# Attention's value products: a step's two of the high part first, the wait for the low part behind them

## The chip, the core and the metric

The kernel runs on one core of one Trainium2 chip. The core has five engines with a queue each: PE (TensorE, matrix products; its weight loads are shown as PEld), DVE (VectorE), ACT (ScalarE), POOL (GpSimd) and SP (SyncE, which here only issues DMAs). An engine takes the instructions of its queue in order, and an instruction waits until the semaphores that it names have reached their values. The metric is the device time of one execution in microseconds (us).

## The reference, cut to what matters

One block of a transformer with conditioning, then a rotation, on x of 4 x 1024 x 576 in float32. The change is in attention: 16 heads of 36 columns, 1024 tokens, four batches, so 64 independent heads.

```python
qkv = h @ W_qkv + b_qkv                     # h: layernorm(x), modulated
q, k, v = (qkv[:, :, 0], qkv[:, :, 1], qkv[:, :, 2])
scores = jnp.einsum('blhd,bmhd->bhlm', q * scale, k)
attn = jax.nn.softmax(scores, axis=-1)
o = jnp.einsum('bhlm,bmhd->blhd', attn, v).reshape(b, l, c)
x = x + gate_msa * (o @ W_proj + b_proj)
```

Around it stand the modulation, the MLP with GELU (576 to 2304 and back) and a rotation of each token by a matrix exponential; the change touches none of them.

## The kernel before, in words

The program runs stage after stage: preparation, q/k/v, attention, projection, MLP, rotation. Attention (`stage_attention`) takes the span from about 650 to 1760 us. Products keep float32's accuracy by splitting an operand into a high part, rounded to the type that PE multiplies, and a low part, the rest; both are multiplied and added up in PSUM.

A head has STEPS = 8 steps. A step handles 256 keys (two tiles of 128) by 512 queries; steps 0 to 3 are the first half of the queries (`lh` 0), 4 to 7 the second. For each head the engines do this:

- PE, `scores` (L1052): two products give the step's scores, keys by queries, into one of two PSUM buffers (`a_psum_t`). The row's maximum is already in the product, through two extra rows of `a_qs`, so its result needs only the exponential. PE runs AHEAD = 3 steps in front with these.
- ACT (L1004, L1006): two exponentials of the buffer, one rounded into `a_ph` (the high part), one in full into `a_pf`, or back into the PSUM buffer in steps 1 and 5. After the second, `exp_done` counts.
- The low part `a_pl` = full less high: POOL does it for steps 0, 2, 3, 4, 6 and 7 (L896, `lo_pool` counts), DVE for steps 1 and 5 (L945, `lo_dve` counts). DVE reads the PSUM buffer, which becomes free for PE's scores two steps on only then (L1045). `a_ph`, `a_pl` and `a_pf` are rings of eight steps.
- PE, `values` (L1071, L1072): four products with the two tiles' values (`a_vs`) as weights, high and low for the first tile, then high and low for the second, all summed in `a_psum_o`. The wait for the low part stands ahead of all four. `p_free` counts when the last is done.
- PE, `score_tile` (L1035): queries by keys of the head after the next, 128 queries by two halves of 512 keys, only to find the maxima; DVE reduces each half (L929), and after tile 7 the pairs to one number a query (L933).
- POOL, `split_max` (L884, L886): splits these maxima, after its low part of step 0; DVE turns them (L940), and SP writes them into the rows of `a_qs` by four DMAs (`put_max`, L800, 2 KB each). PE's scores of a head's step 0 wait for that (`max_in`, L1049). In SP's queue `put_max` stands behind the output of the head before (L822, L823) and one more row copy (L835), and ahead of the loads of a later head (L789, L792).
- DVE copies the head's result out of PSUM (L952, L957).

PE's order in a step is written out: scores of three steps on, values of this step, one score tile. POOL's and DVE's orders are written out too; `heads` runs the body as a loop over four heads at a time (SLOTS = 4), with a branch at its end. Lines in the profile are those of this listing.

Of the kernel before, what the change touches and what calls it, by code (L numbers as in the profile page):

```python
# [37 lines left out]
GT = 512  # L38
# [652 lines left out]
def stage_attention(nc, q_s, k_s, v_s, o_t, sums, ada, gates2, x2_s, rsums, wproj, b_proj, early):  # L691
# [5 lines left out]
    KT = L // P  # L697
    LH = L // GT
    PAIR = 2
    STEPS = LH * KT // PAIR  # L700
# [5 lines left out]
    RING = 8  # L706
# [3 lines left out]
    VW = VLO + D  # L710
# [9 lines left out]
    with ExitStack() as ctx:  # L720
# [6 lines left out]
        vs = sb("vs", [P, SLOTS, KT, VW], F32R)  # L727
        pf = sb("pf", [P, RING, COLS])
        ph = sb("ph", [P, RING, COLS], F32R)
        pl = sb("pl", [P, RING, COLS], F32R)  # L730
# [13 lines left out]
        p_o = ps("o", [P, LH, GT])  # L744
# [12 lines left out]
        exp_done, lo_pool, lo_dve = sem("exp_done"), sem("lo_pool"), sem("lo_dve")  # L757
# [11 lines left out]
        def heads(eng, body):  # L769

            n = NHEAD // SLOTS
            with eng.Fori(0, n - 1) as i:
                for u in range(SLOTS):
                    body(SLOTS * i + u, u, i, False)
            for u in range(SLOTS):
                body(SLOTS * (n - 1) + u, u, n - 1, True)

        def lo_counts(n_heads, s):

            d = sum(x <= s for x in DVE_LO)  # L780
            return NPOOL * n_heads + s + 1 - d, NDVE * n_heads + d

        with nc.Block() as block:
# [226 lines left out]
            @block.tensor  # L1010
            def _(pe):
                pe.sem_inc(p_free, RING)

                def score_product(out, u, t):

                    for h in range(L // 512):
                        m = pe.matmul(out[:, h * 512:(h + 1) * 512], qs[0:SROWS, u, t * P:(t + 1) * P],
                                      ks[0:SROWS, u, h * 512:(h + 1) * 512], start=True, stop=True)
                    m.then_inc(s_ready, 1)

                def lead_tile(n):
                    u, t = divmod(n, KT)
                    if t == 0:
                        pe.wait_ge(qk_in[u], 16 * QK_LOADS)
                    if n >= 3:
                        pe.wait_ge(s_free, n - 2)
                    score_product(lead_slots[n % 3], u, t)

                def score_tile(hd, u, i, t):

                    if t == 0:
                        pe.wait_ge(qk_in[u], 16 * QK_LOADS * (i + 1))
                    for h in range(2):
                        pe.wait_ge(half_free, 2 * (KT * (hd - 2) + t) + h + 1)
                        pe.matmul(p_s[:, h * 512:(h + 1) * 512], qs[0:SROWS, u, t * P:(t + 1) * P],  # L1035
                                  ks[0:SROWS, u, h * 512:(h + 1) * 512], start=True, stop=True) \
                          .then_inc(half_ready, 1)

                def scores(hd, u, i, s):

                    lh, j = divmod(s, PER_LH)
                    if s == 0:
                        pe.wait_ge(max_in[u], START + 64 * (i + 1))
                    if s >= 2 and s - 2 in DVE_LO:
                        pe.wait_ge(lo_dve, lo_counts(hd, s - 2)[1])  # L1045
                    elif isinstance(hd, int) and hd == 0 and s < 2:
                        pe.wait_ge(s_free, LEAD - 2 + s)
                    else:
                        pe.wait_ge(exp_done, STEPS * hd + s - 1)  # L1049
                    for r in range(PAIR):  # L1050
                        t = PAIR * j + r
                        m = pe.matmul(p_t[:, s % 2, r * GT:(r + 1) * GT], ks[0:MROWS, u, t * P:(t + 1) * P],  # L1052
                                      qs[0:MROWS, u, lh * GT:(lh + 1) * GT], start=True, stop=True)
                    m.then_inc(t_ready, 1)

                def values(hd, u, i, s):

                    lh, j = divmod(s, PER_LH)
                    if s == 0:
                        pe.wait_ge(v_in[u], 16 * V_LOADS * (i + 1))  # L1060
                    if j == 0:
                        pe.wait_ge(o_copied[lh], START + hd)
                    n_pool, n_dve = lo_counts(hd, s)
                    if s in DVE_LO:
                        pe.wait_ge(lo_dve, n_dve)
                    else:
                        pe.wait_ge(lo_pool, n_pool)
                    for r in range(PAIR):
                        t = PAIR * j + r
                        cols = slice(r * GT, (r + 1) * GT)  # L1070
                        pe.matmul(p_o[0:VW, lh], vs[:, u, t], ph[:, s % RING, cols], start=(t == 0), stop=False)  # L1071
                        m = pe.matmul(p_o[0:VW, lh], vs[:, u, t], pl[:, s % RING, cols], start=False,  # L1072
                                      stop=(t == KT - 1))
                    m.then_inc(p_free, 1)

                for n in range(LEAD):
                    lead_tile(n)
                for s in range(AHEAD):
                    scores(0, 0, 0, s)
                pe.wait_ge(s_free, LEAD)  # L1080

                def body(hd, u, i, last):
                    for s in range(STEPS):
                        if s + AHEAD < STEPS:
                            scores(hd, u, i, s + AHEAD)
                        elif not (last and u == SLOTS - 1):
                            scores(hd + 1, (u + 1) % SLOTS, i + (u == SLOTS - 1), s + AHEAD - STEPS)
                        values(hd, u, i, s)
                        if not (last and u >= SLOTS - 2):
                            score_tile(hd + 2, (u + 2) % SLOTS, i + (u + 2) // SLOTS, s)  # L1090

                heads(nc.tensor, body)
# [1260 lines left out]
```

## Time and profile before

| | us |
|---|---|
| median of 3 runs | 3061.78 (3058.14 to 3062.56) |
| the profiled execution | 3062.73 |
| its span, first to last instruction | 3061.1 |
| PE busy | 2805.0 (92%) |
| DVE busy | 1680.9 (55%) |
| POOL busy | 1437.3 (47%) |
| ACT busy | 1416.8 (46%) |
| L1071 and L1072, value products, 1024 each | 420.9 and 405.1 |
| L896, POOL's low parts, 384 | 908.6 |

The busy shares are means over stages that differ: ACT and POOL have most of their work in attention. A product's time in the trace runs to its modelled end, and the next one starts before that, so products are counted here by the distance between their starts. A wait is the idle time of an engine just before an instruction, with the instruction that released it.

### The profile page before, as it was taken

What the parts mean: (1) busy time and instruction counts of PE and PEld (TensorE: products, weight loads), DVE (VectorE), ACT (ScalarE), POOL (GpSimd) and SP (SyncE); (2) the same over time, 40 slices, a digit from 0 to 9 for tenths busy, and PEclk for the clock granted to TensorE, in tenths of its full rate; (3) what the DMA queues carried; (4) which work ended last, traced back from release to release, by engine and by line L of the source; (5) the groups of instructions that cost most, each with busy time, mean ns of one, the idle gap of its engine ahead of it and who ended that gap; (6) DMA issues with size and microseconds to landing.
All of it is one profiled execution on the core that took longest, in us unless ns stands there. A gap on an engine that the chain in (4) does not pass through costs nothing. (4 is left out here: it accounts for less than half of the span.)

```text
span 3061.1 us, 51443 instructions
## 1 busy us (share of the span) xinstructions
PE 2805.0 (92%) x16066; PEld 2272.3 (74%) x16066; DVE 1680.9 (55%) x3417; ACT 1416.8 (46%) x1835; POOL 1437.3 (47%) x1073
## 2 busy tenths in 40 slices
PE   7859999969999999999999879689999999999977
PEld 3248878846666666666666568589999999999976
DVE  4446777558999999999999657511111111111126
ACT  2112322229999999999999836511111111111112
POOL 1232333128888888888888836512222222222210
PEclk8769999979999999999999989899999999999989
DMA  5476675653443434343343259892112111211126
GB/s 191 136 245 228 228 249 196 234 170 85 89 93 83 95 81 94 85 90 91 85 96 81 71 165 289 246 310 74 37 38 66 46 38 37 74 38 37 53 74 217
DMA packets 336907, 377.68 MB, mean 123 GB/s; under 512 B 162816, under 2 KB 226952, under 8 KB 336764
## 3 DMA queue, kind: packets, MB, share of 16 engines
q1 hardware_dynamic: 327162, 356.66, 39.0%
q0 software_dynamic: 4224, 9.44, 1.7%
q10 hardware_dynamic: 5382, 9.67, 1.0%
q8 instruction: 95, 1.56, 0.2%
q14 instruction: 44, 0.36, 0.0%
HBM read 225.77 MB, written 158.93 MB: 126 GB/s over the span
## 5 line engine op out<-in xcount | busy, mean ns | idle before, releaser
L896 POOL TENSOR_TENSOR a_pl<-a_pf,a_ph 128x1024 fp32r<-128x1024 f32 x384 | 908.6, 2401 | 24.8 <-ACT a_pf L1006 24.8
L929 DVE TENSOR_REDUCE a_mx<-a_psum_s 128x1 f32<-128x512 f32 x992 | 637.5, 684 | 92.4 <-PE a_psum_s L1035 88.5
L1004 ACT ACTIVATE a_ph<-a_psum_t 128x1024 fp32r<-128x1024 f32 x512 | 525.9, 1027 | 133.6 <-PE a_psum_t L1052 126.5
L1607 POOL TENSOR_TENSOR m_al<-m_af,m_ah 128x256 fp32r<-128x256 f32 x288 | 211.1, 733 | 760.1 <-DVE m_ah L1616 760.1
L1655 PE MATMUL m_psum_h<-m_ht,m_w 128*128 128x256 f32 x4032 | 528.1, 283 | 30.2 <-DMA m_w<-w_s 20.5
L1616 DVE CAST m_ah<-m_af 128x256 fp32r<-128x256 f32 x288 | 85.1, 295 | 830.2 <-ACT m_af L1593 830.2
L1655 PEld LDWEIGHTS m_psum_h<-m_ht,m_w 128*128 128x128 f32 x4032 | 504.3, 189 | 33.7 <-issue 32.9
L1593 ACT ACTIVATE m_af<-m_psum_h,m_bias 128x256 f32<-128x256 f32 x288 | 136.4, 473 | 826.7 <-PE m_psum_h L1655 826.7
L1669 PE MATMUL m_psum_y<-m_w,m_ah 128*128 128x288 f32 x2304 | 506.7, 295 | 1.6 <-DVE m_y L1633 1.5
L1071 PE MATMUL a_psum_o<-a_ph,a_vs 128*100 128x512 f32 x1024 | 420.9, 411 | 22.4 <-POOL a_pl L896 18.9
L1072 PE MATMUL a_psum_o<-a_pl,a_vs 128*100 128x512 f32 x1024 | 405.1, 396 | 0.0
L1006 ACT ACTIVATE a_pf<-a_psum_t 128x1024 f32<-128x1024 f32 x384 | 391.2, 1019 | 0.0
L1669 PEld LDWEIGHTS m_psum_y<-m_w,m_ah 128*128 128x128 f32 x2304 | 388.1, 188 | 3.4 <-DVE m_y L1633 2.8
L1052 PE MATMUL a_psum_t<-a_qs,a_ks 110*128 110x512 f32 x1024 | 337.9, 412 | 37.8 <-DVE a_pl L945 31.3
L1669 PE MATMUL m_psum_y<-m_w,m_al 128*128 128x288 f32 x1152 | 341.3, 296 | 0.0
L1035 PE MATMUL a_psum_s<-a_ks,a_qs 108*128 108x512 f32 x992 | 313.9, 397 | 2.5 <-DVE a_mx L929 2.4
L1071 PEld LDWEIGHTS a_psum_o<-a_ph,a_vs 128*100 128x100 f32 x1024 | 168.7, 165 | 150.1 <-POOL a_pl L896 99.7
L1052 PEld LDWEIGHTS a_psum_t<-a_qs,a_ks 110*128 110x128 f32 x1024 | 184.5, 191 | 122.6 <-DVE a_pl L945 82.9
L663 PE MATMUL q_psum_pqk<-q_ht,q_w 128*128 128x512 f32 x1008 | 257.9, 408 | 13.3 <-DMA q_bv<-in_L_cond_b_qkv_dram 13.3
L1035 PEld LDWEIGHTS a_psum_s<-a_ks,a_qs 108*128 108x128 f32 x992 | 188.3, 190 | 64.9 <-DVE a_mx L929 3.6
L663 PEld LDWEIGHTS q_psum_pqk<-q_ht,q_w 128*128 128x128 f32 x1008 | 188.1, 192 | 55.6 <-issue 13.7
L1669 PEld LDWEIGHTS m_psum_y<-m_w,m_al 128*128 128x128 f32 x1152 | 216.6, 188 | 0.0
(232 smaller groups left out, 3059.5 us busy)
## 6 DMA issues: line engine op xcount, KB each, us to landing
a_qs<-q_s SPq DMA_DIRECT2D x192, 144.0 KB
a_ks<-k_s SPq DMA_DIRECT2D x192, 144.0 KB
w_s<-q_ws SPq DMA_DIRECT2D x64, 324.0 KB, 3.5
h_s<-p_ht SPq DMA_DIRECT2D x40, 512.0 KB, 4.7
m_ht<-h_s SPq DMA_DIRECT2D x16, 1280.0 KB, 8.2
v_s<-q_vo SPq DMA_DIRECT2D x64, 288.0 KB, 2.3
a_vs<-v_s SPq DMA_DIRECT2D x128, 144.0 KB, 4.5
q_s<-q_qko SPq DMA_DIRECT2D x32, 512.0 KB, 2.7
```

What stands on the lines that cost most here:

```text
L663: i = pe.matmul(pqk[:, m % 3], w[:, k, m * P:(m + 1) * P], ht[:, half, a, :], start=(n == 0), stop=(n == len(PASSES) - 1))
L896: pool.tensor_tensor(pl[:, s % RING], pf[:, s % RING], raw(ph[:, s % RING]), ALU.subtract).then_inc(lo_pool, 1)
L929: dve.tensor_reduce(mx[:, u % 2, t, h:h + 1], p_s[:, h * 512:(h + 1) * 512], AX.X, ALU.max) \
L1004: act.activation(ph[:, s % RING], p_t[:, s % 2], ACT.Exp, scale=SCALE)
L1006: act.activation(full, p_t[:, s % 2], ACT.Exp, scale=SCALE).then_inc(exp_done, 1)
L1035: pe.matmul(p_s[:, h * 512:(h + 1) * 512], qs[0:SROWS, u, t * P:(t + 1) * P], ks[0:SROWS, u, h * 512:(h + 1) * 512], start=True, stop=True) \
L1052: m = pe.matmul(p_t[:, s % 2, r * GT:(r + 1) * GT], ks[0:MROWS, u, t * P:(t + 1) * P], qs[0:MROWS, u, lh * GT:(lh + 1) * GT], start=True, ...
L1071: pe.matmul(p_o[0:VW, lh], vs[:, u, t], ph[:, s % RING, cols], start=(t == 0), stop=False)
L1072: m = pe.matmul(p_o[0:VW, lh], vs[:, u, t], pl[:, s % RING, cols], start=False, stop=(t == KT - 1))
L1607: pool.tensor_tensor(al[:, f % RING], af[:, f % RING], raw(ah[:, f % RING]), ALU.subtract).then_inc(lo_ready, 1)
L1655: m = pe.matmul(p_h[:, f % RING, 0:GM], w1[:, k, f * P:(f + 1) * P], ht[:, q, a], start=(i == 0), stop=(i == len(PASSES) - 1))
L1669: m = pe.matmul(p_y[:, t, a, 0:HALF], part[:, f % RING, t * P:(t + 1) * P], w2[:, s, f, a * HALF:(a + 1) * HALF], start=(f == 0 and i == 0 ...
```

## The change

`values` first waits for the step's exponentials (`exp_done`) and issues the two products of the high part, then waits for the low part and issues the two of the low part. Sum, operands and number of products stay.

```diff
@@ -1060,6 +1060,11 @@
                         pe.wait_ge(v_in[u], 16 * V_LOADS * (i + 1))
                     if j == 0:
                         pe.wait_ge(o_copied[lh], START + hd)
+                    pe.wait_ge(exp_done, STEPS * hd + s + 1)
+                    for r in range(PAIR):
+                        t = PAIR * j + r
+                        pe.matmul(p_o[0:VW, lh], vs[:, u, t], ph[:, s % RING, r * GT:(r + 1) * GT],
+                                  start=(t == 0), stop=False)
                     n_pool, n_dve = lo_counts(hd, s)
                     if s in DVE_LO:
                         pe.wait_ge(lo_dve, n_dve)
@@ -1067,10 +1072,8 @@
                         pe.wait_ge(lo_pool, n_pool)
                     for r in range(PAIR):
                         t = PAIR * j + r
-                        cols = slice(r * GT, (r + 1) * GT)
-                        pe.matmul(p_o[0:VW, lh], vs[:, u, t], ph[:, s % RING, cols], start=(t == 0), stop=False)
-                        m = pe.matmul(p_o[0:VW, lh], vs[:, u, t], pl[:, s % RING, cols], start=False,
-                                      stop=(t == KT - 1))
+                        m = pe.matmul(p_o[0:VW, lh], vs[:, u, t], pl[:, s % RING, r * GT:(r + 1) * GT],
+                                      start=False, stop=(t == KT - 1))
                     m.then_inc(p_free, 1)
 
                 for n in range(LEAD):
```

On PE's queue, step 4 of a head, whose low part comes from POOL (`a_o_copied1` is DVE's copy of the head before; `a_psum_s` are score tiles), before:

```order
L1052 MATMUL a_psum_t<-a_qs,a_ks 128x512 [waits a_lo_dve]
L1052 MATMUL a_psum_t<-a_qs,a_ks 128x512
L1067 REGISTER_ALU [waits a_o_copied1]
L1071 MATMUL a_psum_o<-a_ph,a_vs 100x512 [waits a_lo_pool]
L1072 MATMUL a_psum_o<-a_pl,a_vs 100x512
L1071 MATMUL a_psum_o<-a_ph,a_vs 100x512
L1072 MATMUL a_psum_o<-a_pl,a_vs 100x512
L1034 ISA
L1035 MATMUL a_psum_s<-a_ks,a_qs 128x512 [waits a_half_free]
L1034 REGISTER_ALU
L1035 MATMUL a_psum_s<-a_ks,a_qs 128x512 [waits a_half_free]
```

And now:

```order
L1052 MATMUL a_psum_t<-a_qs,a_ks 128x512 [waits a_lo_dve]
L1052 MATMUL a_psum_t<-a_qs,a_ks 128x512
L1066 MATMUL a_psum_o<-a_ph,a_vs 100x512 [waits a_exp_done,a_o_copied1]
L1066 MATMUL a_psum_o<-a_ph,a_vs 100x512
L1072 REGISTER_ALU
L1075 MATMUL a_psum_o<-a_pl,a_vs 100x512 [waits a_lo_pool]
L1075 MATMUL a_psum_o<-a_pl,a_vs 100x512
L1034 ISA
L1035 MATMUL a_psum_s<-a_ks,a_qs 128x512 [waits a_half_free]
L1034 REGISTER_ALU
L1035 MATMUL a_psum_s<-a_ks,a_qs 128x512 [waits a_half_free]
```

The wait for `a_lo_pool` has moved from the first value product to the third, the second tile's high product has moved ahead of the first tile's low one, and a wait for `a_exp_done` stands on the first.

The next step, 5, whose low part comes from DVE, before:

```order
L1043 ISA
L1049 ISA [waits a_max_in0]
L1052 MATMUL a_psum_t<-a_qs,a_ks 128x512 [waits a_exp_done]
L1052 MATMUL a_psum_t<-a_qs,a_ks 128x512
L1071 MATMUL a_psum_o<-a_ph,a_vs 100x512 [waits a_lo_dve]
L1072 MATMUL a_psum_o<-a_pl,a_vs 100x512
L1071 MATMUL a_psum_o<-a_ph,a_vs 100x512
L1072 MATMUL a_psum_o<-a_pl,a_vs 100x512
```

And now:

```order
L1043 ISA
L1049 ISA [waits a_max_in0]
L1052 MATMUL a_psum_t<-a_qs,a_ks 128x512 [waits a_exp_done]
L1052 MATMUL a_psum_t<-a_qs,a_ks 128x512
L1063 REGISTER_ALU
L1066 MATMUL a_psum_o<-a_ph,a_vs 100x512 [waits a_exp_done]
L1066 MATMUL a_psum_o<-a_ph,a_vs 100x512
L1075 MATMUL a_psum_o<-a_pl,a_vs 100x512 [waits a_lo_dve]
L1075 MATMUL a_psum_o<-a_pl,a_vs 100x512
```

The wait for `a_lo_dve` has moved in the same way, and one register instruction (L1063, which works out the value to wait for) is new. In four heads PE's queue has 17 such instructions more.

## Rows read from the trace of the kernel before

**Rows 1.** Busy us, 700:1700; columns PE, PEld, DVE, ACT, POOL, clock, DMA

```profile
700.00:1700.00 1000.00, 956.93 (x3818) 649.94 (x3816) 910.07 (x1433) 908.15 (x955) 866.95 (x478) 1.00 0.39 88
```

**Rows 2.** Waits, 700 to 1700 us; columns: us in total, times, longest

```profile
POOL a_mh L884 <- DVE a_mf L933: 126.1, 59, 2.2
PEld a_psum_o L1071 <- POOL a_pl L896: 92.5, 179, 0.7
...
DVE a_mx L929 <- PE a_psum_s L1035: 80.8, 179, 0.5
PEld a_psum_t L1052 <- DVE a_pl L945: 73.2, 119, 0.9
```

**Rows 3.** POOL in order of time; columns: start, us, engine and line, idle before

```profile
1005.90 0.19 POOL L884 CAST a_mh<-a_mf 128x8 fp32r<-128x8 f32 x1 [2.14 <-DVE a_mf L933]
...
1006.34 14.21 POOL L896 TENSOR_TENSOR a_pl<-a_pf,a_ph 128x1024 fp32r<-128x1024 f32 x6
1022.68 0.19 POOL L884 CAST a_mh<-a_mf 128x8 fp32r<-128x8 f32 x1 [2.13 <-DVE a_mf L933]
...
1023.11 2.41 POOL L896 TENSOR_TENSOR a_pl<-a_pf,a_ph 128x1024 fp32r<-128x1024 f32 x1
```

**Rows 4.** PE in order of time over the same head

```profile
1004.39 0.73 PE L1052 MATMUL a_psum_t<-a_qs,a_ks 110*128 110x512 f32 x2 [0.42 <-DVE a_pl L945]
...
1008.81 0.47 PE L1071 MATMUL a_psum_o<-a_ph,a_vs 128*100 128x512 f32 x1
1009.12 0.40 PE L1072 MATMUL a_psum_o<-a_pl,a_vs 128*100 128x512 f32 x1
...
1009.82 0.63 PE L1035 MATMUL a_psum_s<-a_ks,a_qs 108*128 108x512 f32 x2
...
1012.73 0.73 PE L1052 MATMUL a_psum_t<-a_qs,a_ks 110*128 110x512 f32 x2
1013.52 0.47 PE L1071 MATMUL a_psum_o<-a_ph,a_vs 128*100 128x512 f32 x1
1013.84 0.39 PE L1072 MATMUL a_psum_o<-a_pl,a_vs 128*100 128x512 f32 x1
...
1016.85 0.63 PE L1052 MATMUL a_psum_t<-a_qs,a_ks 110*128 110x512 f32 x2
1017.32 0.40 PE L1071 MATMUL a_psum_o<-a_ph,a_vs 128*100 128x512 f32 x1
...
1018.25 0.63 PE L1035 MATMUL a_psum_s<-a_ks,a_qs 108*128 108x512 f32 x2
```

**Rows 5.** DVE in order of time over the same head

```profile
1010.25 1.29 DVE L929 TENSOR_REDUCE a_mx<-a_psum_s 128x1 f32<-128x512 f32 x2 [0.48 <-PE a_psum_s L1035]
1011.46 1.22 DVE L945 TENSOR_TENSOR a_pl<-a_psum_t,a_ph 128x1024 fp32r<-128x1024 f32 x1
...
1018.69 1.29 DVE L929 TENSOR_REDUCE a_mx<-a_psum_s 128x1 f32<-128x512 f32 x2 [0.39 <-PE a_psum_s L1035]
1019.89 1.22 DVE L945 TENSOR_TENSOR a_pl<-a_psum_t,a_ph 128x1024 fp32r<-128x1024 f32 x1
...
1022.34 0.17 DVE L933 TENSOR_REDUCE a_mf<-a_mx 128x8 f32<-128x16 f32 x1
```

**Rows 6.** ACT in order of time, the same head

```profile
1009.80 1.01 ACT L1006 ACTIVATE a_psum_t<-a_psum_t 128x1024 f32<-128x1024 f32 x1
```

**Rows 7.** SP's queue in order of time, this head and the next

```profile
1010.33 2.64 SPq L800 DMA_DIRECT2D a_qs<-a_mt  x4
...
1027.57 2.67 SPq L800 DMA_DIRECT2D a_qs<-a_mt  x4
```

**Rows 8.** Issues of line 800; columns: duration in ns, least, median, most

```profile
L800 SPq DMA_DIRECT2D a_qs<-a_mt x241: 610/611/705, 689.9 to 1699.7; - x121
```

**Rows 9.** PE's weight loads in order of time, the next head

```profile
1031.52 0.42 PEld L1052 LDWEIGHTS a_psum_t<-a_qs,a_ks 110*128 110x128 f32 x2
```

**Rows 10.** DMA from 1030.5 to 1031.5 in 40 slices, busy tenths

```profile
DMA  0000000000000001110000000000000000000009
```

## The prediction

> **What bounds the kernel now.** I read the busy table of the attention stretch first, then its waits, then the engines' order of time over one head. The table shows no engine full: PE 957 of 1000 us, DVE 910, ACT 908, POOL 867, the granted clock 1.00, which is the 2.4 GHz level [rows 1]. So a loop of waits sets the pace, not one engine, and the waits show which: POOL waits 59 times for DVE's row maxima, 126.1 us in all; PE's weight loads wait 179 times (three a head) for POOL's low parts and 119 times (two a head) for DVE's; DVE waits 179 times for PE's score tiles [rows 2].
>
> One head is one turn of that loop. POOL starts the split of the maxima at 1005.90 and again at 1022.68, so a head takes 16.77 us [rows 3]. I follow the turn edge by edge, counting the head's eight steps from 0:
> - POOL, 7.57 us: the two small splits, then low parts one after another. Six take 14.21 us and one 2.41, so they start (14.21 - 2.41) / 5 = 2.36 apart; the third one (step 4) ends at 1006.34 + 2 x 2.36 + 2.41 = 1013.47 [rows 3].
> - PE, 4.73 us: step 4's first value product starts at 1013.52, the score tile of step 6 at 1018.25 [rows 4]. The product after a stop begins 0.31 us before the next one (1008.81 to 1009.12) where the pitch is 0.232 (1013.84 to 1018.25 is 19 products), so a stop costs 0.08 more. 0.08 + 20 x 0.232 = 4.72: no gap is left in it.
> - PE to DVE 0.44 us; DVE 3.65 us: two maxima, the low part of the next head's step 1 at 1019.89, two maxima, the last reduction at 1022.34 [rows 5]; 0.34 us to POOL's next split.
> The sum is 7.57 + 0.05 + 4.73 + 0.44 + 3.65 + 0.34 = 16.78. It closes: this is the loop that binds, and step 4's four value products are on it as a block behind POOL's low part.
>
> **The change part by part.** It moves two products of four from behind the wait to ahead of it, in each of 512 steps; no product, load or element is added.
> - *Step 4, on the path.* When the low part lands at 1013.47 only the two low products are left. The path from there to the score tile of step 6 has 18 products, not 20: 2 x 0.232 = 0.465 us less a head. PE can have done the high ones by then: its score products start at 1012.73 [rows 4], with 0.10 for a restarted load the next slot is at 1013.29, and two products more end their slots at 1013.76; that is 0.16 past the 1013.60 at which the low products could start, so at the old phase PE would be the later one. This asks for the second loop:
> - *The loop of PE and DVE without POOL.* DVE's low part frees PE's score buffer at 1004.39; from there 22 products (0.10 + 22 x 0.232 = 5.20 us) lead to the score tile of step 2, at 1009.59 if nothing stops PE. The row says 1009.82, so POOL's wait at 1008.81 costs 0.23 in it. DVE needs 0.43 + 1.21 + 1.22 us to the end of its low part of step 5 and PE restarts at 1012.73; from there the same 22 products would give 1017.93 and the row says 1018.25 [rows 4, 5]: 0.32 more for POOL at 1013.52. Both stops go with the change, because the high products fill them (0.47 us is more than either). Its length is 16.77 - 0.23 - 0.32 = 16.22. It is shorter than 16.77 - 0.465 = 16.31, so POOL's loop still sets the pace, with only 0.09 to spare, and the 0.16 above is absorbed: after some heads PE and DVE run that much earlier against POOL.
> - *The added waits.* Each high product's load now waits for the exponential of its own step, finished about three steps earlier: PE's score product three steps on already waited for that of the step after it. Nothing is behind it. A load with a wait already met costs nothing: step 6's first product carries POOL's wait, long met, and starts at 1017.32, two pitches after the pair at 1016.85 [rows 4]. I take 0. The upper bound is the restart, 0.08 a load; a gain is excluded, since an extra wait removes no work. The order also has 17 more register instructions on PE's queue in four heads; the score tiles of before have such instructions between their products, and these follow at the same 0.232 in the 19 of 1013.84 to 1018.25, so I take 0 here too, within the same bound.
> - *ACT as cover.* The exponential for step 5's low part ends at 1009.80 + 1.01 = 1010.81 [rows 6], DVE took it at 1011.46; when the loop loses 0.23 ahead of it, 0.4 is left. ACT follows PE's score products and moves with them.
> - *What is late next: the maxima's transfer.* SP sends them in four DMAs behind the previous head's output; PE's scores of the next head's step 0 wait for them. The tightest are those behind the branch at which the loop over four heads turns round: there SP starts them at 1027.57, 17.24 after the head before (1010.33) instead of 16.77. The last of the four is issued at 1027.57 + 2.67 - 0.61 = 1029.63 (0.61 is one issue) [rows 7, 8], its packets lie in the 15th to 18th slice of 1030.5 to 1031.5, so up to 1030.95 [rows 10], and PE's load that needs it starts unhindered at 1031.52 [rows 9]. So the slack there is between 0 and 0.57 us, and in the other heads, by the 1010.33, 0.47 more. The change brings the needing load 0.465 closer to the sending end, which follows DVE's chain. The lateness is thus 0 to 0.465 in 15 heads: 0 to 7.0 us. I take the middle of the slack, 0.28, since no row is nearer to either end: 0.19 x 15 = 3 us lost.
> The Trainium skill ("DMA: Bandwidth & Descriptors", section "Anatomy of one DMA — SWDGE (gpsimd) path") gives a DMA that POOL issues a fixed cost of about 2.0 us, most of it until the last byte is confirmed. If the same held for SP's, by that estimate the last DMA would land at about 1031.63, the slack would be nothing and the sum would lose the full 7 us, which is rival 1. The trace has at most 1.89 us from issue to use, a little less than the figure.
>
> **The sum.** The pattern holds for 59 to 60 of the 64 heads (59 waits of POOL, 179 / 3 of PE [rows 2]); I take 60: 60 x 0.465 = 27.9 us. Less 3 for the transfer: 24.9. The stage's last step also has two products fewer after its low part: 0.5, and the ramp of the first two heads is left at nothing. 25.4 us. The profiled execution took 3062.73 us (span 3061.1 and 1.6 around it); it becomes 3037.3. That execution lies 0.95 above the median of the runs, 3061.78; so the forecast is 3036.4, rounded to 3037.
>
> **The rivals.**
> 1. *The transfer of the maxima takes the wait over in full.* For: the slack may be 0 [rows 7 to 10]. One head in four then keeps its 16.77: 45 x 0.465 = 20.9 us gained, 3041. If the delay carries into the neighbours, half of the gain goes: 3048. Against: no PE wait on it stands in the list of waits of this stretch [rows 2].
> 2. *Nothing happens*, because POOL's wait is for DVE, which is 91% busy, and DVE's own order sets it: 3062. For: DVE idles only 3 x 80.8 / 179 = 1.35 us a head in front of its maxima [rows 2]. Against: the waits in front of the very reductions of this loop (0.48 and 0.39 us) are released by PE [rows 5], so earlier tiles are taken earlier.
> 3. *Slower: the weight loads lose their cover.* There are 16 waiting value loads a head now, 8 before. If each of the eight added ones is held back until the product ahead of it is over, it costs the restart, 0.08: 8 x 0.08 = 0.64 a head against 0.465, 60 x 0.175 = 10.5 us more, 3072. It decides from 0.465 / 8 = 0.058 us a load on. Against: the met wait at 1017.32 costs nothing [rows 4].
> 4. *More than forecast*: if POOL's low parts come a little faster as well, the second loop binds: 62 x 0.55 = 34 us (64 heads less two of the ramp), 3028. Against: nothing here touches POOL's 2.36.
>
> **How the numbers follow.** The forecast, with the transfer late by little, 3030 to 3040: 0.60. Rival 1, 3040 to 3050: 0.21. Rival 2: 0.07. Rival 3: 0.05. Rival 4: 0.04. Between 3050 and 3056: 0.03. The range 3029 to 3050 holds 0.83 of this; all of it lies on one side. About 0.2% (6 us) is what a measurement of this kernel can tell from no change: faster 0.88, same 0.07, slower 0.05.
>
> **What would show it.** POOL's wait for the maxima falls from 2.13 to about 1.67 us and its period from 16.77 to 16.3 to 16.4; six low parts still take 14.21. PE's loads of the low products, not of the high ones, wait for POOL, and by less in sum than 0.5 us a head; PE's waits for DVE's low part stay. DVE's 0.48 before its maxima shrinks. In one head of four a wait of PE on the maxima's DMA of 0.1 to 0.3 us may appear. I am wrong if the period is above 16.5 or if products after a met wait start more than 0.25 apart.

## The result, and the profile after

The changed kernel takes **3027.84 us** (median of 4 runs, 3024.55 to 3031.68), the kernel before, timed beside it, 3059.96 (4 runs, 3054.84 to 3062.56): a ratio of 0.9898, with an interval of 0.9879 to 0.9916. The forecast was 3037 us with a range of 3029 to 3050. The direction was right; the time lies 9 us below the forecast and 1.2 us below the range.

The same kernel timed again in two later series gave 3032.13 (5 runs), which lies in the range, and 3025.80 (4 runs). All 13 runs have the median 3028.64; the 47 runs of the kernel before that stood beside the experiments have 3054.66. The change is worth about 26 us.

The profiled execution of after takes 3028.64 us (span 3027.0). First its attention stretch, in the columns of [rows 1]:

```profile
700.00:1700.00 1000.00, 959.70 (x3889) 660.69 (x3888) 926.60 (x1459) 924.38 (x975) 885.11 (x488) 1.00 0.40 90
```

All engines are a little busier than before, DVE 927 against 910 us, because more heads fit into 1000 us: POOL has 488 instructions there instead of 478. No engine is full, and the granted clock is the same 1.00.

The waits of the same stretch, to be held against [rows 2]:

```profile
POOL a_mh L884 <- DVE a_mf L933: 99.2, 58, 2.0
PEld a_psum_t L1052 <- DVE a_pl L945: 88.7, 121, 0.9
...
DVE a_mx L929 <- PE a_psum_s L1035: 56.8, 180, 0.9
PEld a_psum_o L1075 <- POOL a_pl L896: 38.6, 121, 1.2
...
PEld a_psum_s L1035 <- DVE a_mx L929: 23.8, 86, 3.1
...
PEld a_psum_t L1052 <- issue: 5.5, 15, 0.4
```

PE's loads wait for POOL's low parts 121 times, not 179, and 38.6 us in all, not 92.5; it is the loads of the low products (line 1075) that wait, the high ones (line 1066) do not stand in the list. POOL's wait for the maxima falls by a fifth, DVE's wait for score tiles by 30%. Two rows have no counterpart in the list of before: 86 waits of the score tiles' loads for DVE's reductions, and 15 waits of the score products' loads, which the profile puts down to "issue". The loads' waits for DVE's low part (line 1052) have grown, from 73.2 to 88.7 us.

POOL in order of time, as in [rows 3]:

```profile
1001.91 0.19 POOL L884 CAST a_mh<-a_mf 128x8 fp32r<-128x8 f32 x1 [1.67 <-DVE a_mf L933]
...
1018.43 0.19 POOL L884 CAST a_mh<-a_mf 128x8 fp32r<-128x8 f32 x1 [1.88 <-DVE a_mf L933]
...
1018.86 14.21 POOL L896 TENSOR_TENSOR a_pl<-a_pf,a_ph 128x1024 fp32r<-128x1024 f32 x6
1034.73 0.19 POOL L884 CAST a_mh<-a_mf 128x8 fp32r<-128x8 f32 x1 [1.66 <-DVE a_mf L933]
...
1051.03 0.19 POOL L884 CAST a_mh<-a_mf 128x8 fp32r<-128x8 f32 x1 [1.67 <-DVE a_mf L933]
```

The heads take 16.52, 16.30 and 16.30 us. Between the ramps at both ends of the stage (where heads take longer) three heads of four take 16.26 to 16.31 and the fourth 16.48 to 16.57, a mean of 16.34 where it was 16.77 [rows 3]. The work of POOL is unchanged: its six low parts still take 14.21.

The same turn can be followed edge by edge again, here on PE from 1025.02, in the form of [rows 4]:

```profile
1025.02 0.73 PE L1052 MATMUL a_psum_t<-a_qs,a_ks 110*128 110x512 f32 x2 [0.17 <-DVE a_pl L945]
1025.59 0.62 PE L1066 MATMUL a_psum_o<-a_ph,a_vs 128*100 128x512 f32 x2
1026.05 0.70 PE L1075 MATMUL a_psum_o<-a_pl,a_vs 128*100 128x512 f32 x2
...
1030.31 0.62 PE L1035 MATMUL a_psum_s<-a_ks,a_qs 108*128 108x512 f32 x2
```

and on DVE, as in [rows 5]:

```profile
1022.55 1.29 DVE L929 TENSOR_REDUCE a_mx<-a_psum_s 128x1 f32<-128x512 f32 x2 [0.24 <-PE a_psum_s L1035]
...
1030.74 1.29 DVE L929 TENSOR_REDUCE a_mx<-a_psum_s 128x1 f32<-128x512 f32 x2 [0.39 <-PE a_psum_s L1035]
...
1034.39 0.17 DVE L933 TENSOR_REDUCE a_mf<-a_mx 128x8 f32<-128x16 f32 x1
```

POOL's third low part (step 4) ends at 1018.86 + 2 x 2.36 + 2.40 = 1025.98, 7.55 after the split began. The low products start at 1026.05, 0.07 later. From there to the score tile at 1030.31 are 4.26 us = 0.08 + 18 x 0.232: 18 products, as forecast, where before there were 20. Then 0.43 to DVE, 3.65 of DVE, 0.34 to POOL. 7.55 + 0.07 + 4.26 + 0.43 + 3.65 + 0.34 = 16.30. POOL's loop still binds, two products shorter. The high products run from 1025.59 to about 1026.05, almost exactly until the low part arrives: the two loops are as close as the prediction had them.

Where the 34.1 us between the two profiled executions lie, marked by the first and last split of the maxima (line 884):

| profiled execution of | to first split | first to last split | behind it | span |
|---|---|---|---|---|
| before | 665.0 | 1067.0 | 1329.1 | 3061.1 |
| after | 653.2 | 1040.7 | 1333.2 | 3027.0 |
| difference | -11.9 | -26.3 | +4.1 | -34.1 |

From the first to the last split the stage gained 26.3 us, against a forecast of 24.9 (the forecast's other 0.5, for the stage's last step, lies behind the last split). 60 heads between the ramps, from the third split on, gained 25.4 of it: 1006.0 to 980.6. The first two heads and the last, which the prediction left at nothing, make up the rest, and they differ as much between executions of one kernel: 61.0 and 60.1 us in two of before, 60.0, 61.6 and 59.6 in three of after. The other 7.8 us lie in stages that the change does not touch; that is followed up below.

### The profile page after: what moved, and what is told of

Same layout as the page of the kernel before. It is cut to its first block and busy times, and to the rows that moved or that the text cites. A ratio compares the mean times of both kernels' runs of the same rounds, so it can differ in the third digit from the quotient of the medians.

```text
span 3027.0 us, 51803 instructions
## 1 busy us (share of the span) xinstructions
PE 2778.0 (92%) x16066; PEld 2268.9 (75%) x16066; DVE 1678.0 (55%) x3417; ACT 1415.1 (47%) x1835; POOL 1437.0 (47%) x1073
## 5 line engine op out<-in xcount | busy, mean ns | idle before, releaser
L1075 PE MATMUL a_psum_o<-a_pl,a_vs 128*100 128x512 f32 x1024 | 329.9, 403 | 2.7 <-POOL a_pl L896 2.7
L1066 PE MATMUL a_psum_o<-a_ph,a_vs 128*100 128x512 f32 x1024 | 321.5, 395 | 0.0
L1075 PEld LDWEIGHTS a_psum_o<-a_pl,a_vs 128*100 128x100 f32 x1024 | 158.7, 165 | 94.1 <-POOL a_pl L896 42.7
```

Source lines behind the costliest of these rows:

```text
L1066: pe.matmul(p_o[0:VW, lh], vs[:, u, t], ph[:, s % RING, r * GT:(r + 1) * GT], start=(t == 0), stop=False)
L1075: m = pe.matmul(p_o[0:VW, lh], vs[:, u, t], pl[:, s % RING, r * GT:(r + 1) * GT], start=False, stop=(t == KT - 1))
```

## The experiments

Two questions: is the gain the loop of the prediction, or something else about the new order; and where does the miss of 9 us come from. The kernels ran in three series, each with runs of the kernel before beside them (medians 3054.47, 3055.26 and 3055.22). Since a time differs by some us from run to run, I read each kernel's loop from its trace as well: first to last split, and the mean length of a head between the ramps.

| kernel | median us (runs) | ratio to before, interval | first split | first to last split | a head |
|---|---|---|---|---|---|
| before again | 3055.23 (12) | 0.9997, 0.9985 to 1.0010 | 652.5 | 1065.9 | 16.76 |
| after again, 1st | 3032.13 (5) | 0.9918, 0.9905 to 0.9931 | 659.3 | 1042.1 | 16.34 |
| after again, 2nd | 3025.80 (4) | 0.9898, 0.9879 to 0.9918 | 653.1 | 1040.8 | 16.35 |
| step 4 alone | 3036.68 (6) | 0.9940, 0.9925 to 0.9954 | 653.2 | 1050.0 | 16.48 |
| all but steps 2 and 4 | 3055.47 (11) | 1.0000, 0.9990 to 1.0009 | 656.9 | 1063.7 | 16.74 |
| steps 2 and 4 alone | 3028.42 (4) | 0.9909, 0.9890 to 0.9928 | 652.6 | 1042.1 | 16.36 |
| one product, not two | 3040.99 (6) | 0.9941, 0.9926 to 0.9957 | 653.0 | 1052.7 | 16.54 |
| after, maxima sent earlier | 3025.71 (4) | 0.9895, 0.9881 to 0.9909 | 665.6 | 1038.3 | 16.285 |
| the same again | 3022.48 (4) | 0.9888, 0.9872 to 0.9905 | 651.4 | 1036.1 | 16.30 |
| before, maxima sent earlier | 3051.73 (10) | 0.9981, 0.9971 to 0.9992 | 659.4 | 1065.8 | 16.76 |
| maxima earlier and split later | 3016.66 (4) | 0.9871, 0.9851 to 0.9890 | 652.5 | 1032.8 | 16.23 |

**Which steps bring it.** The prediction says that only two steps of eight count: step 4, whose products lie on POOL's loop, and step 2, where POOL's stop lengthens the loop of PE and DVE. Three kernels keep the new order in some steps and the old one in the rest. This is the first of them; the second has `(0, 1, 3, 5, 6, 7)` in the first line and the third `(2, 4)`:

```diff
+    HIGH_FIRST = (4,)
...
+                    if s in HIGH_FIRST:
+                        pe.wait_ge(exp_done, STEPS * hd + s + 1)
+                        for r in range(PAIR):
+                            product(ph, r, False)
...
                     for r in range(PAIR):
+                        if s not in HIGH_FIRST:
+                            product(ph, r, False)
+                        m = product(pl, r, PAIR * j + r == KT - 1)
```

Step 4 alone:

> The high products come first in step 4 alone. Theory of the two loops: POOL's loop loses its 0.465 us, but the loop of PE and DVE keeps POOL's stop at step 2 (0.23 us) and sets the pace: 16.4 to 16.5 us a head, 19 us faster than before, with PE stopped for POOL at steps 2 and 3 and not at 4. Rival (each of the three stops that PE makes for POOL is worth its own length): a third of the gain or less, 16.6 us a head, 9 us. Rival (the gain comes from the order in all eight steps): an eighth, 3 us.

It gained 16 to 17 us between first and last split, at 16.48 us a head, and the ratio is 0.9940. The loads of the value products still wait for POOL twice a head, at steps 2 and 3 (columns as in [rows 2]; most lines of this kernel are numbered one higher, and line 1066 stands for all its value products):

```profile
PEld a_psum_o L1066 <- POOL a_pl L897: 63.9, 120, 0.7
```

PE in order of time shows what the one that counts, step 2's, costs:

```profile
1004.21 0.72 PE L1053 MATMUL a_psum_t<-a_qs,a_ks 110*128 110x512 f32 x2 [0.42 <-DVE a_pl L946]
...
1008.61 0.47 PE L1066 MATMUL a_psum_o<-a_ph,a_vs 128*100 128x512 f32 x1
1008.93 0.39 PE L1066 MATMUL a_psum_o<-a_pl,a_vs 128*100 128x512 f32 x1
...
1009.63 0.62 PE L1036 MATMUL a_psum_s<-a_ks,a_qs 108*128 108x512 f32 x2
```

From 1004.21, 22 products unhindered (0.10 + 22 x 0.232 = 5.20) would reach the score tile at 1009.41; it starts at 1009.63. The loop of PE and DVE, 16.22, with these 0.22 is 16.44 long, 0.04 under what was measured, and so it binds before POOL's loop gets to 16.31. The second loop of the prediction is real, and step 4 alone cannot bring the whole gain.

All but steps 2 and 4:

> The high products come first in steps 0, 1, 3, 5, 6 and 7, not in 2 and 4. Theory: nothing of the two loops is touched, 16.77 us a head, 0 us (the last step's two products: 0.5 us). Rival (added waits and register instructions cost the restart, 0.08 us): six such steps are 0.5 us a head, 29 us slower than before. Rival (the gain comes from the order of products itself): six eighths of it, 20 us faster.

Six steps of eight in the new order bring nothing that the time shows (1.0000, 0.9990 to 1.0009). POOL's wait is what it was before, 2.11 us (line 885 is 884 in the kernels before and after):

```profile
1012.89 0.19 POOL L885 CAST a_mh<-a_mf 128x8 fp32r<-128x8 f32 x1 [2.11 <-DVE a_mf L934]
1029.63 0.19 POOL L885 CAST a_mh<-a_mf 128x8 fp32r<-128x8 f32 x1 [2.12 <-DVE a_mf L934]
```

It also shows that the added waits of rival 3 cost nothing that the time shows: six of the eight steps with them are in this kernel. Its head is 0.02 to 0.03 us shorter than that of before; what gives that I did not find.

Steps 2 and 4 alone:

> The high products come first in steps 2 and 4 alone. Theory of the two loops: POOL's loop loses its 0.465 us by step 4 and the loop of PE and DVE loses POOL's two stops, so all of the gain is there: 16.28 us in three heads of four and 16.50 in the fourth, attention 1089 us, 25 us faster. Rival (the gain grows with the number of steps): a quarter of it, 6 us, or with step 3 missing two thirds, 17 us.

3028.42 us, and 1042.1 from first to last split where the full change has 1040.7 to 1042.1: two steps of eight bring all of the gain.

```profile
1001.23 0.19 POOL L885 CAST a_mh<-a_mf 128x8 fp32r<-128x8 f32 x1 [1.67 <-DVE a_mf L934]
1017.73 0.19 POOL L885 CAST a_mh<-a_mf 128x8 fp32r<-128x8 f32 x1 [1.88 <-DVE a_mf L934]
1034.04 0.19 POOL L885 CAST a_mh<-a_mf 128x8 fp32r<-128x8 f32 x1 [1.66 <-DVE a_mf L934]
```

The first of these heads takes 16.50, the next 16.31: the pattern of after.

**One product instead of two.** If the price is the number of products behind the low part, moving one of the two must bring half, whatever else the order does:

```diff
+                    pe.wait_ge(exp_done, STEPS * hd + s + 1)
+                    product(ph, 0, False)
...
+                    product(pl, 0, False)
+                    product(ph, 1, False)
+                    m = product(pl, 1, PAIR * j + 1 == KT - 1)
```

> In every step only the first tile's high product stands ahead of the wait, the second one stays between the two low ones. Theory of the two loops: POOL's loop has 19 products where before had 20, so it loses 0.232 us and stays the longer one: 16.77 - 0.23 = 16.54 us a head, the same in all heads since the maxima then still arrive in time; 14 us faster in all, attention 1102 us. Rival (what counts is that each stop of PE is filled, the longest being 0.41 us): one product fills over half of them, 16.4 us a head or less, 20 us and more.

The heads take 16.51 to 16.58, mean 16.54, and 16.77 - 0.232 = 16.54. The price of a product behind the wait is its pitch.

```profile
1005.01 0.19 POOL L884 CAST a_mh<-a_mf 128x8 fp32r<-128x8 f32 x1 [1.91 <-DVE a_mf L933]
1021.52 0.19 POOL L884 CAST a_mh<-a_mf 128x8 fp32r<-128x8 f32 x1 [1.88 <-DVE a_mf L933]
```

No fourth head is longer here: 0.23 us less does not yet make the maxima's transfer late. In the kernel with step 4 alone, at 0.29 less, the list of waits does have 15 named "issue", of at most 0.2 us (2.9 us in all), and the fourth heads are longer by only about 0.04.

**The maxima's transfer.** In after every fourth head is 0.22 us longer. The prediction expected this, by its slack of 0 to 0.57 us in the head that follows the loop's branch. PE's weight loads and SP's queue of after there, as in [rows 9] and [rows 7]:

```profile
1010.62 0.30 PEld L1052 LDWEIGHTS a_psum_t<-a_qs,a_ks 110*128 110x128 f32 x2 [0.37 <-issue]
```

```profile
1006.81 2.67 SPq L800 DMA_DIRECT2D a_qs<-a_mt  x4
...
1023.01 2.66 SPq L800 DMA_DIRECT2D a_qs<-a_mt  x4
```

The last of the four DMAs is issued at 1006.81 + 2.67 - 0.61 = 1008.87, and the load that had been waiting starts 1.75 us later. The profile names no DMA as what ended the wait. On PE the delay is smaller than among the loads:

```profile
1009.54 0.68 PE L1075 MATMUL a_psum_o<-a_pl,a_vs 128*100 128x512 f32 x2
1010.06 0.64 PE L1035 MATMUL a_psum_s<-a_ks,a_qs 108*128 108x512 f32 x2
1010.63 0.72 PE L1052 MATMUL a_psum_t<-a_qs,a_ks 110*128 110x512 f32 x2
...
1014.01 0.62 PE L1035 MATMUL a_psum_s<-a_ks,a_qs 108*128 108x512 f32 x2
```

Two pitches after 1010.06 the score products would start at 1010.52; they start at 1010.63, 0.11 late, and the restart costs 0.10 more. From step 4's low products to step 6's score tile are 4.47 us here, not 4.26: these 0.21 are what the head is longer by. The rest of the load's 0.37 lay beside products that were running.

The test sends the maxima earlier: SP makes the row copy that stood behind the two stores (line 835) ahead of them, so that the maxima of the next head stand behind less.

```diff
                         load(hd + SLOTS - 1, (u + SLOTS - 1) % SLOTS)
+                    sp.wait_ge(rows_out, 16 * B)
+                    sp.dma_start(x2_s[bass.ds(hd * SHARE, SHARE)], ...)
                     for lh in range(LH):
                         store(hd, lh)
-                    sp.wait_ge(rows_out, 16 * B)
-                    sp.dma_start(x2_s[bass.ds(hd * SHARE, SHARE)], ...)
```

> The changed kernel with SP's row copy of a head moved ahead of its two outputs, so that the next head's maxima leave 0.72 us earlier (1010.33 less 1009.61 before). Theory (the transfer of the maxima is what makes one head in four take 16.50 us and not 16.28): all heads 16.28 us, 15 x 0.22 = 3 us faster than the changed kernel. Rival (the longer head comes from the branch at the loop's end on PE or POOL itself): one head in four stays at 16.50 us, no difference.

All heads between the ramps take 16.25 to 16.31 now, mean 16.28, and the "issue" row is gone from this kernel's list of waits:

```profile
1014.47 0.19 POOL L884 CAST a_mh<-a_mf 128x8 fp32r<-128x8 f32 x1 [1.65 <-DVE a_mf L933]
1030.75 0.19 POOL L884 CAST a_mh<-a_mf 128x8 fp32r<-128x8 f32 x1 [1.65 <-DVE a_mf L933]
```

So the wait named "issue" was the transfer, and it costs 15 x 0.22 = 3.3 us in after. The same was run once more:

> The changed order with the maxima sent earlier, once more, for the interval: 16.28 us in all heads, attention 1086 to 1088 us, 27 to 30 us faster than the kernel before and 3 us faster than the changed kernel. Rival (the first comparison was luck): no difference to the changed kernel.

16.30 us in all heads, 1036.1 from first to last split, 4.7 us less than after in the same series. In the 60 heads between the ramps alone the two executions with the earlier transfer are 3.4 and 3.3 us shorter than after in their series (977.1 against 980.4, 977.9 against 981.2), which is the 3.3. And the move by itself, in the kernel before:

> The kernel before with SP's row copy moved behind the loads, so that the maxima leave 0.72 us earlier, and the value products as they were. Theory: the maxima arrive 0.2 us and more ahead of need in the kernel before, so sending them earlier brings nothing: 16.77 us a head, 0 us. Rival (the row copy's place costs time by itself): 3 us faster as beside the changed order.

The loop is what it was, 16.76 us a head and 1065.8 from first to last split, as expected. But the time is lower than that of before, 0.9981 (0.9971 to 0.9992), 3.5 us. The expectation's rival had named such a gain; it lies outside the loop. The profiled execution has 1327.0 us behind the last split where the other one of before in this series has 1333.6; the four profiled executions with the earlier transfer have 1326.6 to 1331.2 there, the nine others 1329.1 to 1336.9. That overlaps. Some 1.3 us of it lies where attention hands over: ACT's first step of the projection (line 1390, 1393 in after, `p_rs`) starts 33.6 us behind the last split here, and 35.1 and 34.9 in the two executions of before; with the changed order 32.6 in both with the earlier transfer and 33.8 to 34.0 in the three without. The last row copy no longer stands between the last output and what SP copies next. The rest stays open. So the run times of the kernels with the earlier transfer hold a gain that is not the loop's, and the price of the transfer is read from the heads.

**What binds next.** If POOL's loop is closed first by the split of the maxima, a split made later in POOL's order takes POOL out of it, and the loop of PE and DVE, 16.22, must remain. POOL turns to the next head's maxima behind step 2's low part instead of step 0's (with the earlier transfer kept):

```diff
-                        if s == 0 and not (last and u == SLOTS - 1):
+                        if s == 2 and not (last and u == SLOTS - 1):
                             split_max(hd + 1, (u + 1) % SLOTS)
```

> The changed order with the maxima sent earlier (as in the second experiment), and POOL's split of the maxima put behind its low part of step 2 instead of step 0. Theory of the two loops: POOL's loop then has one low part fewer behind the maxima (2.36 us less) and binds no more; the loop of PE and DVE alone is left, whose length was worked out at 16.22 us: 16.20 to 16.25 us a head in all heads, POOL without a wait for the maxima, PE without stops for POOL, 2 to 5 us faster than with the maxima sent earlier alone. Rival (16.28 us is the loop of PE and DVE already): no difference. Rival (POOL's later split makes DVE's turn and the transfer late): 16.4 us and more.

The heads take 16.22 to 16.25, POOL no longer waits for the maxima but for ACT, and PE does not wait for POOL any more. POOL in order of time, and the waits over 700 to 1700 us:

```profile
1005.49 7.21 POOL L896 TENSOR_TENSOR a_pl<-a_pf,a_ph 128x1024 fp32r<-128x1024 f32 x3 [0.67 <-ACT a_pf L1006]
...
1015.86 0.19 POOL L884 CAST a_mh<-a_mf 128x8 fp32r<-128x8 f32 x1
...
1032.10 0.19 POOL L884 CAST a_mh<-a_mf 128x8 fp32r<-128x8 f32 x1
```

```profile
PEld a_psum_t L1052 <- DVE a_pl L945: 99.8, 123, 1.9
POOL a_pl L896 <- ACT a_pf L1006: 95.4, 125, 2.3
...
DVE a_mx L929 <- PE a_psum_s L1035: 49.9, 179, 0.9
```

The loop of PE and DVE closes in this kernel, here from PE and DVE in order of time:

```profile
1013.27 0.73 PE L1052 MATMUL a_psum_t<-a_qs,a_ks 110*128 110x512 f32 x2 [0.41 <-DVE a_pl L945]
...
1018.47 0.74 PE L1035 MATMUL a_psum_s<-a_ks,a_qs 108*128 108x512 f32 x2
...
1021.38 0.73 PE L1052 MATMUL a_psum_t<-a_qs,a_ks 110*128 110x512 f32 x2 [0.28 <-DVE a_pl L945]
```

```profile
1020.11 1.22 DVE L945 TENSOR_TENSOR a_pl<-a_psum_t,a_ph 128x1024 fp32r<-128x1024 f32 x1
```

From 1013.27 to 1018.47 are 5.20 us, the 22 products without a stop; DVE's low part starts 1.64 later and takes 1.22, and PE goes on 0.05 after it. That is 8.11 us for one of the head's two low parts of DVE, and twice that is 16.22.

3016.66 us, 0.9871 of before (0.9851 to 0.9890): this version beats both kernels. It is 9 us below after and 6 below the kernel with the earlier transfer alone, both in the same series; 2 to 5 was expected of the latter, and 3.9 lie in the 60 heads between the ramps (977.9 to 974.0). The 16.22 that the prediction had worked out from before's trace, by taking two stops out of a loop, is the length that this kernel shows.

**The miss of 9 us.** The kernels before and after were run again, unchanged, for a second and third profile:

> The kernel before, once more. Theory: attention takes 1116 us in this profiled execution too (16.77 us a head), while the preparation differs from the 158 us of the first profile by several us, as it did among the changed kernels (149 to 162 us); the difference of medians to the kernel before is 0 within 3 us. Rival (the preparation is long because of this kernel's program): 158 us again.

> The changed kernel once more, word for word. Theory: attention alone gains, 27.4 us as its first trace has it (from 1116.3 to 1088.8 us), and the rest of the 34 us between the two profiled executions is spread of the other stages between executions (preparation 8.2 us shorter, projection and MLP 5.9 longer), so the difference of the medians settles at 25 to 29 us and the preparation lies anywhere from 150 to 160 us. Rival: the change also shortens what stands before attention by its place in the program: the difference stays at 32 to 34 us and the preparation at 150 to 152 us again.

> The changed kernel a third time, on the chip of the two others: 16.28 us in three heads of four and 16.50 in the fourth, attention 1089 to 1091 us, 24 to 28 us faster than before. Of the preparation: where the granted clock from 20 to 145 us is near 0.80 it takes 156 to 162 us, where it is near 0.88 it takes 149 to 151.

The differences of the medians, 22.3 and 29.4 us for the two of after and 0.0 for before, leave the expected 25 to 29 and 24 to 28 on either side. The stretch from first to last split repeats: 1067.0 and 1065.9 for before, 1040.7, 1042.1 and 1040.8 for after. What precedes it does not: the kernel before begins its attention at 665.0 in one profiled execution and at 652.5 in the other, after at 653.2, 659.3 and 653.1. I had guessed that TensorE's granted clock in the preparation (20 to 145 us) decides it; the kernel with step 4 alone began at 653.2 with a granted clock of 0.82 there, hardly above the 0.80 of before, so by that window the guess failed. The products themselves tell more. The groups of the preparation's conditioning products, first in before and then in after (columns: count; busy us, mean ns of one; idle before):

```profile
L2225 PE MATMUL c_psum_v<-c_wa,c_sct 128*4 128x432 f32 (+1 forms) x80 | 42.3, 634 | 0.0
L2253 PE MATMUL c_psum_b<-x_m,c_sel 64*64 64x128 f32 x128 | 34.8, 362 | 17.0 <-DVE x_m L2131 15.4 <-DVE c_sct L2121 0.9
L2225 PE MATMUL c_psum_v<-c_wt,c_sct 128*4 128x504 f32 x32 | 21.1, 748 | 0.0
```

```profile
L2228 PE MATMUL c_psum_v<-c_wa,c_sct 128*4 128x432 f32 (+1 forms) x80 | 36.6, 558 | 1.7 <-DMA c_wa<-in_L_cond_b_ada_dram 1.7
L2256 PE MATMUL c_psum_b<-x_m,c_sel 64*64 64x128 f32 x128 | 32.1, 337 | 15.3 <-DVE x_m L2134 13.4 <-DVE c_sct L2124 0.9
...
L2228 PE MATMUL c_psum_v<-c_wt,c_sct 128*4 128x504 f32 x32 | 19.1, 683 | 0.0
```

The same 80 products take 634 ns each in one and 558 in the other. The three groups sum to 98.2 and 87.8 us of busy time: the difference, 10.4, is near the 11.9 us by which attention starts later. Over the thirteen profiled executions this sum and the first split go together: 87.0 to 89.3 us with 651.4 to 653.2 (eight of them), 94.3 with 656.9, 96.2 with 659.3 and 659.4, 98.2 with 665.0, 100.9 with 665.6. The granted clock of the first 200 us, busy us of the engines as in [rows 1], in before and in after:

```profile
0.00:200.00 200.00, 139.04 (x473) 53.59 (x474) 83.13 (x270) 33.09 (x50) 46.49 (x50) 0.74 0.57 186
```

```profile
0.00:200.00 200.00, 139.34 (x520) 60.47 (x520) 87.54 (x280) 36.69 (x57) 48.82 (x52) 0.80 0.59 194
```

It is 0.74 in the four with the latest first split, 0.77 at 656.9 and 0.78 to 0.80 in the other eight. Of the two levels, 1.2 and 2.4 GHz, the lower one was granted longer there. That this is what makes the products longer fits the rows, but no run changes the clock alone, so it is not shown; nor does any run tell what makes one execution get more of the lower level than another.

## Why the prediction missed

- **What binds, and the term of the change: right.** POOL's loop was to lose 2 x 0.232 = 0.465 us a head. It lost 0.47 to 0.49 (16.77 to 16.28 or 16.30), by 18 products in place of 20; one product alone brought 0.23. Steps 2 and 4 alone brought all, the six others nothing.
- **The second loop: right.** 16.22, forecast from two stops in the trace of before, is what the loop takes once POOL is out of it (16.23), and with the stop at step 2 left it is 16.48, against 16.22 + 0.22 = 16.44. Of PE's three stops a head for POOL only step 2's is gone from the list of after: the loads wait 121 times, two a head, 0.64 us a head in sum where the prediction's sign was less than 0.5. That sign failed. The wait that is left at step 4 is the one on POOL's loop, whose 0.08 the 4.26 us hold.
- **Added waits, loads and register instructions at nothing: right.** The kernel with six of eight added waits is at 1.0000 of before. Rival 3, at 3072, is out.
- **The maxima's transfer: right in place, and in size by luck.** 0.22 us in every fourth head, 3.3 us in 15 heads; the forecast took 3, but as the middle of 0 to 7 because no row was nearer to either end, and half of the 0.21 seen on PE is a restart, which the term did not have. Rival 1, a full loss of 7 us and more, did not come: the load waits until 1.75 us after the start of the last issue. The Trainium skill ("DMA: Bandwidth & Descriptors", section "Anatomy of one DMA — SWDGE (gpsimd) path") has about 2.0 us of fixed cost for a DMA that POOL issues; these are SP's, and the trace has less.
- **The attention stage in sum:** -26.3 us against -24.9. Of the difference, 0.5 lies in the 60 heads (25.4 against 24.9) and 1 in the ramps, put at nothing, where executions of one kernel differ by as much.
- **The step that failed: the base.** "That execution lies 0.95 above the median of the runs, 3061.78; so the forecast is 3036.4." The three runs behind that median, 3058 to 3063, were high ones: the 47 later runs of the same kernel have the median 3054.66 and go from 3048.77 to 3066.29. The profiled execution lies 8 us above that, not 0.95, and the trace shows where: its preparation took some 12 us more than that of the second profile. 3054.66 - 25.4 = 3029.3, which is 0.6 above the median of all runs of after, 3028.64. The gain was forecast to within 1 us; it was subtracted from an execution with a slow preparation. Of the miss of 9.2 us, 7.1 is the base (3061.78 against 3054.66), 0.6 the gain, 0.6 the rounding of 3036.4 to 3037, and 0.8 that the four runs of the result lie under the median of all 13. Only 12 of the 47 runs lie at 3058 or above; why three in a row did at first, no run tells.
- **The range followed from the same step.** It held what was unknown in the loop, 3029 to 3050, and nothing for the stages outside, which differ by up to 14 us between executions ahead of attention and by 10 behind it (1326.6 to 1336.9). Its chance was 0.83, where the classes that lie in it sum to 0.81. Rival 4's time, 3028, is what came, but not by its mechanism: the second loop does not bind in after.

## What to carry to other kernels

Close the binding loop edge by edge until its sum is the period; then an instruction that is moved out from behind a wait is worth its pitch where the wait is on that loop, and nothing elsewhere (two steps of eight here). Work out the length of the next loop as well, by taking from it the stops that go: it says how far the change can carry, and what to move next. And before a gain is subtracted from a profiled execution, compare that execution's other stages with more than three runs: here the stages that nothing had changed moved the time by as much as a third of the gain.

## What was not expected of the hardware

- A wait for a small transfer within the core was listed as "issue": 15 waits, 5.5 us. Only moving the transfer showed what it was. The waiting load starts 1.75 us after the start of the last issue.
- A weight load that waited 0.37 us cost the loop 0.22 us: 0.11 by which PE's next product came late and 0.10 for the restart; the rest of the wait lay beside running products.
- The products of 432 columns in the preparation took from 557 to 668 ns each in executions of kernels that are the same there, with granted clocks of 0.74 to 0.80 over the first 200 us, and moved the start of attention by up to 14 us. Inside attention the granted clock was 1.00 in each kernel quoted above, and a head repeated within some hundredths of a us.
